# Attention scores by 32x32 tiles, state read out beside them, masked scores spread through DRAM, every engine in a new order

## Time and profile before

| | us |
|---|---|
| median of 3 executions (1781.02 to 1781.83) | 1781.47 |
| profiled execution | 1783.68 |
| its span, first to last instruction | 1781.9 |
| mean granted TensorE clock | 0.966 |
| PE busy | 1658.3 |
| DVE busy | 1303.9 |
| ACT busy | 1009.2 |
| POOL busy | 858.7 |

### The profile page before, as it was taken

One profiled execution on the slowest core, in us unless ns is written; L12 is line 12 of the kernel. 1 busy time (PEld: TensorE's weight loads), 2 busy tenths in 40 slices (PEclk: granted clock), 3 DMA queues, 4 the chain that ended last, 5 costly groups with the idle time before them and its releaser, 6 DMA issues.

```text
span 1781.9 us, 47524 instructions
## 1 busy us (share of the span) xinstructions
PE 1658.3 (93%) x15176; PEld 1406.3 (79%) x15176; DVE 1303.9 (73%) x4558; ACT 1009.2 (57%) x3694; POOL 858.7 (48%) x1293
## 2 busy tenths in 40 slices
PE   5488899999999999999999999999999999998876
PEld 3377788888888888888888888888888888887755
DVE  4456677787777777877778777787777777776554
ACT  4355566666565665655656656556566666554431
POOL 1355355554554555545545655455455554443211
PEclk8689899999999999999999999999999999999878
DMA  4211111011111110011111110111111101110000
GB/s 121 66 31 31 31 32 27 26 25 35 35 35 35 33 26 25 22 35 35 35 35 35 25 27 23 31 35 35 35 35 28 25 23 30 31 31 7 6 7 12
DMA packets 108174, 56.26 MB, mean 32 GB/s; under 512 B 73904, under 2 KB 107344, under 8 KB 107984
## 3 DMA queue, kind: packets, MB, share of 16 engines
q1 hardware_dynamic: 106464, 53.75, 11.8%
q10 hardware_dynamic: 1648, 1.72, 0.3%
HBM read 30.28 MB, written 16.78 MB: 26 GB/s over the span
## 4 chain that ended last, share of the span: by engine, by line
PE 76%; ACT 7%; DVE 5%; issue 5%; POOL 4%; DMA 1%; SPq 1%; ACTq 0%; POOLq 0%; DVEq 0%
PE ps L1130 57%; PE ps L1136 5%; PE ps L1173 4%; PE ps L1147 3%; PE ps L1198 2%; PE ps L1163 2%; PE ps L1161 2%; POOL r L386 1%; ACT ym L545 1%; PE ps L1417 1%; DVE hs L772 1%; DVE st L782 1%; PE ps L1193 1%; ACT ps L551 1%; ACT part L557 1%
## 5 line engine op out<-in xcount | busy, mean ns | idle before, releaser
L1130 PE MATMUL ps<-we,yT 128*128 128x512 f32 x3072 | 823.1, 412 | 0.0
L1130 PEld LDWEIGHTS ps<-we,yT 128*128 128x128 f32 x3072 | 548.4, 192 | 101.7
L539 ACT ACTIVATE h_lead<-ps 48x8 fp32r<-48x8 f32 x1024 | 174.4, 170 | 601.3 <-PE ps L1147 595.2
L772 DVE SCALAR_TENSOR_TENSOR hs<-ps,cst,h_lead 48x8 fp32r<-48x8 f32 x1024 | 222.7, 217 | 188.5 <-ACT ps L540 184.2
L1147 PEld LDWEIGHTS ps<-hs,aT 128*128 128x128 f32 x1024 | 196.2, 192 | 104.4 <-DVE hs L772 78.1
L1147 PE MATMUL ps<-hs,aT 128*128 128x8 f32 x1024 | 208.4, 204 | 38.5 <-DVE hs L772 37.9
L803 DVE SCALAR_TENSOR_TENSOR stage<-ps,coef,stage 128x256 f32<-128x256 f32 x384 | 184.1, 479 | 36.8 <-PE ps L1130 24.0
L414 POOL TENSOR_TENSOR part<-part 128x256 f32<-128x256 f32 x64 | 46.7, 730 | 332.7 <-ACT part L558 332.7
L803 DVE SCALAR_TENSOR_TENSOR acc<-ps,coef,acc 128x256 f32<-128x256 f32 x384 | 183.8, 479 | 12.4 <-POOL acc L416 5.3
L436 POOL TENSOR_TENSOR orstd<-omean,mhalf 128x32 f32<-128x32 f32 x32 | 174.1, 5440 | 2.7
L540 ACT ACTIVATE ps<-ps 48x8 f32<-48x8 f32 x1024 | 164.3, 160 | 0.0
(11 more groups left out here) (179 smaller groups left out, 3340.1 us busy)
## 6 DMA issues: line engine op xcount, KB each, us to landing
xin<-in_x SPq DMA_DIRECT2D x64, 128.0 KB
vrow<-vtok SPq DMA_DIRECT2D x32, 256.0 KB, 2.2
vx<-vrow SPq DMA_DIRECT2D x128, 64.0 KB, 2.0
sx<-smid SPq DMA_DIRECT2D x128, 64.0 KB
xag<-in_x SPq DMA_DIRECT2D x64, 128.0 KB
out<-stage SPq DMA_DIRECT2D x64, 128.0 KB
stage<-in_experts SPq DMA_DIRECT2D x1, 2048.0 KB, 8.9
stage<-in_Wvg SPq DMA_DIRECT2D x1, 512.0 KB, 5.3
```

Source lines behind the costliest of these rows:

```text
L539: a.activation(h_lead[:], ps[0:NB, BANK["RB"], k * B:(k + 1) * B], ACT.Tanh)
L772: v.scalar_tensor_tensor(hs[0:NB, :, k], h_whole, keeps_rest, h_lead[:].bitcast(F32), ALU.mult, ALU.subtract).then_inc(sem("rnn_h"), 1)
L1130: ins = t.matmul(dst, left(lp, c), right(rp, c), start=(n == 1), stop=(n == 3 * chunks))
```

## The change

- `scores` swaps the operands: k (32x32) is the weight, and q masked by head (`qx`, 128 columns) moves. Output partitions are now 32 keys per sequence; both tiles' scores stand together. `qx` takes the place of `kx` on ACT, after `qt`.
- `read_state`: q (32x32) as weights, `smid` moving (64 columns), 32 matmuls, into the scores' banks. ACT's `read_out` copies the result into bank O in two instructions. The `sx` products and the spread of `smid` are gone.
- DVE masks the scores in two instructions. SP writes them to DRAM (`arow`, 512 KB) and reads them back by head (`atx`) in four DMAs; `attend` uses `atx`, in the same stage as the scores, in two stretches instead of four.
- The gate: ACT computes |z + bias| and exp of its negative; DVE's instruction goes.
- PE's body is turned: it begins at the former step 25, and what stood before is at the end, one stage lower. On the way VG0 moves ahead of TR, OG behind step 31, Y0 behind T1, attend behind `G1_3` and `G1_4`. The bodies of ACT, DVE and POOL are turned and reordered too. DVE's `gTs` goes from between states 29 and 30 to between 31 and 0; on ACT both `read_out` and tanh 6 go ahead of ym1.
- The fill: `xag` of round 0 is loaded at the start; x of round 1 goes ahead of 12 of the late weight pieces; the experts are split in halves in bodies 3 and 4.

```diff
+        load_x(xag, 0, "x_again")
-            for dst, src in late_sync:
+            for dst, src in late_sync[:6]:
...
-            def spread_state():
+            def spread_scores():
+                for h in range(HQ):
+                    sp.dma_start(atx[h * TS:(h + 1) * TS], arow[:, :, h, :].rearrange("b s c -> s b c")).then_inc(sem("att_spread"), 16)
...
-                    sp.wait_ge(sem("smid"), copied)
-                    spread_state()
+                    sp.wait_ge(sem("att"), masked)
+                    sp.dma_start(arow.rearrange("(i q) s h c -> (q s) i (h c)", q=BQ), att[:].rearrange("p i h c -> p i (h c)")).then_inc(sem("att_out"), 16)
...
+                    sp.wait_ge(sem("att_out"), kept)
+                    spread_scores()
...
+            def read_out(j):
+                o = TOK + TILES * HQ * DV
+                return a.activation(ps[:, BANK["O"], :].rearrange("p (i j c) -> p j i c", i=TILES, j=J)[:, j:j + 2],
+                                    ps[:, SD + j:SD + j + 2, o:o + TILES * HQ * DV].rearrange("p j (i c) -> p j i c", i=TILES), ACT.Copy)
...
-                    state_of(11, c6)
+                    state_of(3, c6)
+                    state_of(4, c6)
+                if live(it, 7):
+                    act.wait_ge(sem("shift_m2"), c7)
+                    normed(m2.y, m2.x, m2.r).then_inc(sem("ym2"), 1)
+                if live(it, 6):
+                    state_of(5, c6)
+                if live(it, 3):
+                    act.wait_ge(sem("DS1"), c3)
+                    act.wait_ge(sem("x3"), past(c7))
+                    act.wait_ge(sem("onorm"), past(c3 - 1))
+                    read_out(2).then_inc(sem("inter"), 1)
+                    act.wait_ge(sem("att"), past(2 * c3 - 1))
+                    read_out(0).then_inc(sem("inter"), 1)
+                if live(it, 6):
+                    state_of(6, c6)
+                if live(it, 5):
+                    act.wait_ge(sem("shift_m1"), c5)
+                    normed(m1.y, m1.x, m1.r).then_inc(sem("ym1"), 1)
...
+                    a.activation(ge[:], ps[:, BANK["Z"], 0:TOK], ACT.Abs, bias=b2g[:, 0:1]).then_inc(sem("nz"), 1)
                     a.activation(zb[:], ps[:, BANK["Z"], 0:TOK], ACT.Identity, bias=b2g[:, 0:1]).then_inc(sem("zb"), 1)
...
+                    a.activation(ge[:], ge[:], ACT.Exp, scale=-1.0).then_inc(sem("ge"), 1)
...
-                    a.activation(ge[:], ge[:], ACT.Exp).then_inc(sem("ge"), 1)
...
+            def mask_scores(j):
+                return v.tensor_tensor(att[:].rearrange("p i h (j t) -> p j (i h) t", j=J)[:, j:j + 2],
+                                       ps[:, SD + j:SD + j + 2, 0:TOK].rearrange("p j (x t) -> p j x t", t=TS),
+                                       causal.unsqueeze(1).unsqueeze(1).broadcast_to([P, 2, B, TS]), ALU.mult)
...
-                    v.tensor_tensor(att[:], ps[:, SD:SD + J, 0:TOK].rearrange("p j (b t) -> p j b t", t=TS),
+                    mask_scores(0).then_inc(sem("att"), 1)
                 if live(it, 5):
                     split_state(5, c5)
                 if live(it, 2):
-                    dve.wait_ge(sem("att"), c2)
+                    dve.wait_ge(sem("inter"), past(2 * c2 - 1))
+                    mask_scores(2).then_inc(sem("att"), 1)
+                    dve.wait_ge(sem("inter"), 2 * c2)
...
-                        ins = t.matmul(ps[:, SD + j, b * TS:(b + 1) * TS], kx[r, b, :, :].rearrange("p h t -> p (h t)"),
-                                       qt[r, b * TS:(b + 1) * TS], start=True, stop=True)
+                        ins = t.matmul(ps[32 * q:32 * q + 32, SD + j, i * P:(i + 1) * P], kt[r, b * TS:(b + 1) * TS],
+                                       qx[r, b, :, :].rearrange("p h t -> p (h t)"), start=True, stop=True)
+            def read_state(i):
...
+                        ins = t.matmul(ps[32 * q:32 * q + 32, SD + j, o:o + HQ * DV], qt[r, b * TS:(b + 1) * TS], smid[r, b, :],
+                                       start=True, stop=True)
```

More of the change, by code:

```diff
@@ L55 @@
 BANK_ORDER = {
[L56 to L61, removed]
@@ L450, in body @@
                     start_acc(m2, 1, c6)
[L451 to L469, removed]
                 if live(it, 0):
@@ L1364, in body @@
-                if live(it, 6):
-                    step(26, c6)
                 if live(it, 2):
@@ L1426, in body @@
                         recurrence_out()
+                if live(it, 5):
+                    if isinstance(it, int) and it == 5:
+                        pe.wait_ge(sem("weights_rest"), REST["recurrence"])
+                    pe.wait_ge(sem("yrT"), c5)
+                    for name, count in readers(it, "RB"):
+                        pe.wait_ge(sem(name), count)
+                    for c in range(KC):
+                        ins = t.matmul(ps[0:NP, BANK["RB"], 0:TOK], bin_[:, c, :], yrT[:, c, :], start=(c == 0), stop=(c == KC - 1), skip_group_check=True)
                 if live(it, 6):
@@ new lines, in body @@
+                if live(it, 5):
+                    step(8, c5)
+                if live(it, 6):
+                    pe.wait_ge(sem("ym2"), c6)
+                    for name, count in readers(it, "T2"):
+                        pe.wait_ge(sem(name), count)
+                    transposed(BANK["T2"], m2.y).then_inc(sem("T2"), 1)
+                if live(it, 4):
+                    pe.wait_ge(sem("yT1"), c4)
+                    for name, count in readers(it, "L1"):
+                        pe.wait_ge(sem(name), count)
+                    logits(m1, BANK["L1"]).then_inc(sem("L1"), 1)
@@ new lines, in body @@
+                if live(it, 5):
+                    step(9, c5)
+                if live(it, 4):
+                    pe.wait_ge(sem("yT1"), c4)
+                    if isinstance(it, int) and it == 4:
+                        pe.wait_ge(sem("weights_rest"), REST["experts"])
+                    for name, count in readers(it, "G1_0"):
+                        pe.wait_ge(sem(name), count)
+                    moe(m1, 0, BANK["G1_0"]).then_inc(sem("moe1"), 1)
+                if live(it, 5):
+                    step(10, c5)
@@ new lines, in body @@
+                if live(it, 5):
+                    step(17, c5)
+                if live(it, 1):
+                    if isinstance(it, int) and it == 1:
+                        pe.wait_ge(sem("weights_rest"), REST["early"])
+                    pe.wait_ge(sem("hTs"), c1)
+                    for name, count in readers(it, "Z"):
+                        pe.wait_ge(sem(name), count)
+                    product(ps[:, BANK["Z"], 0:TOK], lambda p, c: wz[:, p, c, :], lambda p, c: hTs[:, p, c, :], KC).then_inc(sem("Z"), 1)
@@ new lines, in body @@
+                if live(it, 5):
+                    step(18, c5)
+                if live(it, 3):
+                    pe.wait_ge(sem("h2Ts"), c3)
+                    for name, count in readers(it, "F1A"):
+                        pe.wait_ge(sem(name), count)
+                    for f in range(0, 2):
+                        ins = product(ps[:, BANK["F1A"], f % 2 * TOK:(f % 2 + 1) * TOK], lambda p, c: wcols(W_1, p, c, FF, f * P, P),
+                                      lambda p, c: h2Ts[:, p, c, :], KC)
```

762 lines of the change are left out of this document (360 added, 402 removed).

## The result

The changed kernel takes 1735.69 us (median of 4 runs, 1734.93 to 1739.34); the kernel before, on the same chip, took 1781.47. The ratio is 0.9745, 95% interval 0.9729 to 0.9761: 46 us faster, where 19.5 were forecast. The profiled execution has a span of 1733.0 us, 48.9 less than the 1781.90 of before. (A fourth execution of the kernel before, disturbed, took 2021.09 us and is left out.)

What follows compares the result with a forecast made beforehand. It took PE as the bound, with DVE equally binding from step 3 to the first router's logits. Rounds -8 and fill -11 gave -19: 1764.7 us profiled, 1762 median; own range 1736 to 1785, 8-in-10 range 1718 to 1794.

Steps and rivals of the forecast that it cites:

- sign of being wrong: PE idle still under 0.6 us and a period near 48.6, or PE waiting for atx in steady rounds.
- The period: One steady round: 50.4 us against 50.70, bounds 49.6 and 51.3; -8 us over 27 rounds.
- PE's work: Per round, 2.1 us less, from scores, sx products, state_update, attend and stretch entries, against new scores and read_state.
- The waits: New PE idle per round: 0.6 us before step 1, 1.9 us in the stretch after step 3.
- A: Recurrence step 31 to step 3: from 8.51 to 7.0 us, with PE waiting for DVE's state 0.
- BC: Step 3 to the end of the first router's logits: stays 8.3 us, bounds 7.65 and 9.1.
- D: The rest of the round, after the first router's logits: from 33.86 to 35.1 us, VG0 in and OG out.
- The fill: Pipeline start: -11 us, bounds -4 and -16, from early xag (8.3), VG0 before OG (2.5), halved experts (1.5), less 1.
- DMA, Abs, drain: Score transfers hidden with 1 to 2 us of cover, absolute value on ACT, pipeline end: 0 each, drain bounds +-3.
- The DRAM rival: Scores reach attend(0) too late through DRAM; at 1.5 us late per round +21, 1803 us; chance 0.12.
- PE-bound all through: PE bounds every stretch, so its saved work counts: whole 1713 us, half 1735; chance 0.17.
- ACT's order: Read_outs and tanh 6 ahead of ym1 cost 0.86 us a round, 1785 us, about no change; chance 0.14.

Runs made afterwards that it cites:

- pool_beside_rest: The changed kernel with one more POOL addition of 128x512 out of SBUF, beside DVE's rest of gTs: 1758.21 us, ratio 0.9854.
- two_updates: The changed kernel with state_update in two stretches of 32 records and the second read_state inside the second F2 product: 1760.84 us, ratio 0.9876.
- abs_on_dve: The changed kernel with the gate's absolute value on DVE again instead of ACT: 1740.72 us, ratio 0.9747.

## Why the prediction was wrong

The direction was right and the time is inside the range of 8 in 10 (1718 to 1794), but 0.3 us outside the bounds of the forecast's own sum (1736 to 1785), and the gain is 2.4 times the forecast. Of the sign of being wrong that it named, the first half came, PE idle under 0.6 us (0.51); the period, 49.49, lies between the 48.6 named there and the 50.1 to 50.7 called right. By its own steps:

- **The period, the step that failed.** "Period: 7.0 + 8.3 + 35.1 = 50.4" measured 6.71 + 7.95 + 34.83 = 49.49. The prediction let only 0.3 us of the work taken from PE through to the period and turned the rest into waits; measured, 1.15 us of work left and the period fell by 1.21. Each stretch was laid out about 0.3 us too long, and 0.9 us over 27 rounds is some 25 of the 30 us between the sum for the profiled execution (-19) and what it gave (-48.9); the rest is the 4.5 that go with the clock between the first RO and the second and the fill's 1.6, less 0.9 in the drain. The bounds, 49.6 to 51.3, just left the truth out.
- **PE's work** was to fall by 2.1 us and fell by 1.15 (busy, against the windows above). By start distances: scores 0.99 instead of 0.75; state_update in one stretch 0.87 instead of 0.54; attend 0.68 and 0.67 instead of 0.60 twice; KT, RB and RO 1.48 instead of 1.31. These 0.9 us were taken as saved and weren't. In BC the layout left PE 6.5 us of work; it has 7.49. The prediction's own rows give 6.9 (8.04 less 0.43, 2 x 0.37, 0.2 of entries and 0.10, plus 0.32), so 0.4 of that was lost in the sum.
- **The waits** were to be 0.6 in A and 1.9 in BC, and are 0.01 and 0.46. The work was mis-sized by 0.95 us and the waits by 2.0, in opposite directions; what is left between them is the 0.9 us of the period, within 0.2.
- **A.** "DVE now has combine 6 and the rest of gTs (0.9 and 1.76)" put state 0 at 3.55 us after step 31. It began at 2.74 (727.91), before the scores ended at 3.15. pool_beside_rest shows why: the 1.76 held for a rest beside POOL's additions, and the change had moved these away, which the diff showed.
- **BC.** The chain was named (x1, statistics, POOL, ACT) but the layout put ym1 behind ACT's read_outs and T1 at 5.35; it is at 4.97. The two read_outs take 0.65 us together, not 0.46 each, and stand where ACT waits for POOL, so the new work ahead of ym1 costs nothing. dstate ended at 4.4, not 4.8, state 7 began at 6.2, not 6.75. After T1, the gap to the logits fell from 2.47 us (768.07 to 770.54) to the 2.07 of the hand-overs, since sx and the attends left it. So BC's gain is that gap's. That the round has a mixed bound, PE in A and D and hand-overs in BC, holds, as two_updates shows.
- **D** came out 0.97 us longer, not 1.24: VG0 in and OG out as forecast (1.13 by start distances), the attention's matmuls 1.35 instead of 1.38, PE's idle 0.04 instead of 0.16, and the steps' 0.1 nowhere in the way.
- **The fill** was right in sum (-11 forecast, -12.6 at the first RO), with some luck in the clock: abs_on_dve, 0.8 us ahead of the changed kernel at 145 us, has its first RO at 185.4, only 9.4 sooner than the kernel before. Of the parts, xag's 8.3 is what the early load gives in the old order (8.0 at the first RO); in the new order it is 2.8, because DVE's turned body takes oss ahead of xhat, which the prediction did not count. Halves 1.5 against 2.0. Of the 5.7 us from the first RO to the second, 4.5 go with the clock (0.90 before and 1.00 after between 200 and 250 us), and were in no term.
- **DMA, Abs, drain** at nothing: right. SP's four issues took 1.78 us, not 2.71, and the cover is 3 us. The DRAM rival fell.
- **The rivals.** PE-bound all through, at half its size, was put at 1735, which is the time measured. That is luck: half of its 57 us and the fill's 11 give 1742, so 1735 does not follow from its terms, and 4.5 us of the measured gain go with the clock. Its reason, PE's work alone, is refuted for BC by two_updates. It holds for A and D. ACT's order did not cost what its rival said: ym1 starts within 0.03 us of POOL's result. The DRAM path did not happen either.
- **The small tiles.** 64 records run at 15.5 ns each (0.99/64) and 13.6 (0.87/64), not at 10 ns throughout. The Trainium skill, "TensorE: Matmul & The Clock Gate" (Part 1), says that start to start doesn't fall under about 25 ns: the trace disagrees, and the rule was rightly set aside.

## What to carry to other kernels

Cut the round at the points where engines meet, and for each stretch write down two numbers: PE's work, from start distances, and the chain of hand-overs that leads to its end. The longer one is the stretch, and only the part of a saving above the other counts. Take a duration only from a row whose neighbours on the other engines are those the new order will have. Before you price a transfer by the wait for it, see what the new order puts ahead of that wait. And where a chain holds the stretch, look for work that can start on a part of its result: the lead products first gave 0.3 us a round here, with the same matmuls.

## What the runs showed of the hardware

- DVE and POOL hold each other up when both add out of SBUF, and the one that starts second pays: with POOL first by 0.04 us, 1.22 us of DVE became 2.08 and POOL kept its 1.04; with DVE first by 0.03 us, DVE kept its 1.22 and POOL's 1.04 became 2.08. DVE operations that read PSUM beside POOL's additions weren't measured alone.
- A row of small matmuls is cheap only at first: 32 of a 32x32 tile take 0.32 to 0.33 us, 64 take 0.87; with 128 columns 32 take 0.43 and 64 take 0.99. The rows below are windows of 0.1 us with the scores' own instructions alone (PE, then weight loads). The loads fall from 33 in a window to 1 after the first half, and are back at 17 0.2 us later. Why isn't settled.

```profile
727.40:727.50 0.10, 0.10 (x21) 0.10 (x33) 1.00 0.46 115
727.50:727.60 0.10, 0.10 (x32) 0.07 (x17) 1.00 0.75 177
727.60:727.70 0.10, 0.10 (x32) 0.07 (x1) 1.00 0.93 213
727.70:727.80 0.10, 0.10 (x26) 0.09 (x6) 1.00 0.50 103
727.80:727.90 0.10, 0.10 (x19) 0.10 (x17) 1.00 0.19 44
```

- The granted clock after the fill (0.84 or 0.96 between 150 and 200 us) went with totals 5 to 9 us apart for the same rounds. Executions of one kernel differ too: 1732.08 us at a mean of 0.970, 1741.1 to 1741.95 at 0.963 to 0.965.
